# Expert weights turned once by DMA transposes from SBUF, instead of in both stages by TensorE

## What is computed

```python
x = x + 0.5 * _L0_ffn_ref(_layernorm(x), w_gate_up, w_proj)     # ternary FFN
x = x + _L0_attn_ref(_layernorm(x), w_qkv, w_out)               # 16 heads
x = x + 0.5 * _L0_ffn_ref(_layernorm(x), w_gate_up, w_proj)
x = x + 0.5 * _L1_ffn_ref(_layernorm(x), gate_w, gate_b, W1, W2, W3, Ws1, Ws2, Ws3)
x = x + _L1_attn_ref(_layernorm(x), W_Q, W_K, W_V)              # retention
x = x + 0.5 * _L1_ffn_ref(_layernorm(x), gate_w, gate_b, W1, W2, W3, Ws1, Ws2, Ws3)
```

```python
h = silu(einsum('td,eid->tei', xt, W1)) * einsum('td,eid->tei', xt, W3)   # 8 experts, 128 wide
y = einsum('tei,edi,te->td', h, W2, dw)                                   # dw: two experts per token
z = silu(xt @ Ws1.T) * (xt @ Ws3.T) @ Ws2.T                               # a ninth, shared
return y + z
```

## Time and profile before

| what | us |
|---|---|
| median of three runs (lowest, highest) | 1695.41 (1694.16, 1696.23) |
| the profiled execution's own time | 1694.91 |
| its span, first to last instruction | 1693.1 |
| TensorE busy | 1626.9, 96% of the span |
| VectorE, ScalarE, GpSimd busy | 1252.6, 1223.6, 1132.0 |
| first expert stage, from its first `up` | 1287.3 to 1443.1 |
| retention | 1443.1 to 1535.2 |
| second expert stage | 1535.8 to 1693.1 |

### The profile page before, as it was taken

One profiled execution on the slowest core, in us unless ns is written; L12 is line 12 of the kernel. 1 busy time (PEld: TensorE's weight loads), 2 busy tenths in 40 slices (PEclk: granted clock), 3 DMA queues, 4 the chain that ended last, 5 costly groups with the idle time before them and its releaser, 6 DMA issues.

```text
span 1693.1 us, 27014 instructions
## 1 busy us (share of the span) xinstructions
PE 1626.9 (96%) x9467; PEld 962.3 (57%) x9467; DVE 1252.6 (74%) x2407; ACT 1223.6 (72%) x1911; POOL 1132.0 (67%) x749
## 2 busy tenths in 40 slices
PE   4998999999999999999999999998999999999998
PEld 2565455555555555555555555554566566676665
DVE  7878777777777677777777777775796777977766
ACT  7867888988988988988888888885655443444432
POOL 1776888888888888888878878874664223663222
PEclk9999999999999999999999999999999999999999
DMA  9013778788779778788788788785001110000101
GB/s 296 1 51 63 139 129 154 128 143 171 126 146 168 125 150 160 129 152 162 125 152 153 125 143 149 131 139 111 1 1 60 55 53 1 1 2 29 29 10 51
DMA packets 580510, 174.07 MB, mean 103 GB/s; under 512 B 543244, under 2 KB 579351, under 8 KB 580247
## 3 DMA queue, kind: packets, MB, share of 16 engines
q1 hardware_dynamic: 580374, 172.33, 52.6%
HBM read 35.94 MB, written 2.10 MB: 22 GB/s over the span
## 4 chain that ended last, share of the span: by engine, by line
PE 78%; DVE 6%; ACT 2%; issue 1%; POOL 1%; SPq 0%; DMA 0%; DVEq 0%; ACTq 0%; POOLq 0%
PE banks L1909 24%; PE banks L1910 24%; PE banks L1911 24%; PE banks L1984 1%; PE banks L1985 1%; DVE X L1750 1%; DVE mo_h L1737 1%; PE banks L2021 1%; DVE nmax L1563 1%; PE banks L2022 1%; PE banks L1919 1%; PE banks L2076 1%; DVE XN L1258 0%; PE banks L2238 0%; DVE x L1264 0%
## 5 line engine op out<-in xcount | busy, mean ns | idle before, releaser
L762 POOL TENSOR_TENSOR Pl<-Pm,Ph 128x1024 f16<-128x1024 f32 x256 | 546.7, 2136 | 46.8 <-ACT Ph L1026 45.8
L1016 ACT ACTIVATE Pm<-banks,nbias,s_scale 128x1024 f32<-128x1024 f32 x256 | 308.1, 1204 | 120.8 <-DVE nbias L1565 120.8
L1563 DVE TENSOR_REDUCE nmax<-banks 128x1 f32<-128x1024 f32 x256 | 312.6, 1221 | 96.8 <-PE banks L1911 95.7
L1026 ACT ACTIVATE Ph<-Pm 128x1024 f16<-128x1024 f32 x256 | 268.5, 1049 | 1.3
L741 POOL TENSOR_TENSOR rp_b<-rp_s,rope 128x512 f32<-128x512 f32 x128 | 163.0, 1273 | 135.6 <-ACT rp_s L993 135.4
L1602 DVE SCALAR_TENSOR_TENSOR X<-banks,rinv,X 128x256 f32<-128x256 f32 x256 | 112.7, 479 | 157.8 <-PE banks L1911 157.8
L818 POOL TENSOR_TENSOR mT_lo<-mo_h,mT_hi 128x512 f16<-128x512 f32 x72 | 83.8, 1164 | 205.8 <-ACT mT_hi L1129 205.5
L1909 PE MATMUL banks<-PT_hi,V_hi 128*128 128x512 f16 x512 | 195.1, 381 | 3.1 <-DMA PT_lo<-Pl 3.1
L1909 PE MATMUL banks<-QK_hi 128*128 128x512 f16 x512 | 195.3, 381 | 1.2 <-DVE QK_lo L1650 1.2
L1910 PE MATMUL banks<-PT_lo,V_hi 128*128 128x512 f16 x512 | 195.1, 381 | 0.0
L1911 PE MATMUL banks<-PT_hi,V_lo 128*128 128x512 f16 x512 | 195.1, 381 | 0.0
(11 more groups left out here) (248 smaller groups left out, 4129.9 us busy)
## 6 DMA issues: line engine op xcount, KB each, us to landing
moe_raw<-in_L_ffn_W SPq DMA_DIRECT2D x72, 128.0 KB, 2.3
w_all<-in_L_attn_w_qkv SPq DMA_DIRECT2D x3, 2048.0 KB, 15.8
a_raw<-in_L_attn_w_qkv SPq DMA_DIRECT2D x24, 256.0 KB, 3.1
PT_hi<-Ph SPq DMA_TRANSPOSE x256, 3.4
PT_lo<-Pl SPq DMA_TRANSPOSE x256, 3.3
raw_gu<-in_L_ffn_w_gate_up SPq DMA_DIRECT2D x2, 1024.0 KB, 7.2
X<-in_L_attn_x SPq DMA_DIRECT2D x2, 1024.0 KB, 12.9
o_raw<-in_L_attn_w_out SPq DMA_DIRECT2D x8, 256.0 KB, 3.4
```

Of the source, the lines that this page charges most:

```text
L762: nc.gpsimd.tensor_tensor(Pl[:, z % 4, :], Pm[:, k, :], Ph[:, z % 4, :], ALU.subtract).then_inc(pl_done.sem, 1)
L1016: nc.scalar.activation(Pm[:, k, :], two_banks[z % 2][:], ACT.Exp, bias=nbias[:, z:z + 1], scale=s_scale[:], accum_out=rsum[:, z:z + 1]).th ...
L1026: nc.scalar.activation(Ph[:, z % 4, :], Pm[:, (base * SLOTS + z) % 3, :], copy).then_inc(ph_done.sem, 1)
L1563: nc.vector.tensor_reduce(nmax[:, z:z + 1], two_banks[z % 2][:], AX, ALU.max, negate=True).then_inc(max_done.sem, 1)
```

## The change

Weights are turned once, in the first expert stage, and kept for the second. ScalarE and VectorE split the raw rows in SBUF into `m16` (high and low part, one buffer); Sync then issues two DMA transposes of 128 x 768 fp16, one for each part, into `w16`, which holds all nine experts. TensorE's `expert_weights` and all waits that belonged to it are gone. The split of weight `q` waits for the transposes of `q - 1`, because `m16` is single. Work for weight 0 moves into the last phase of the FFN, and the later weights move to other steps. In the second expert stage no weight is loaded, split or turned. `r_raw`, `xpos`, `decay` and `at_hi` change their addresses in SBUF; the last two mixes of the retention return to banks 6 and 7.

```diff
-    w13_hi, w13_lo, w2_hi, w2_lo = [], [], [], []
...
+    w16 = sb("w16", [P, NX, 2, 3, D], fp16)
...
+    m16 = sb("m16", [P, 2, 3, D], fp16)
...
-        WEIGHTS_AFTER = {0: 2, 7: 3, 13: 4, 15: 5, 17: 6, 20: 7, 24: 8}
+        WEIGHTS_AFTER = {0: 2, 4: 3, 7: 4, 9: 5, 13: 6, 16: 7, 18: 8}
...
-        MIX_BANK = [(4, 5, 6, 7, 4, 5, 6, 7), (4, 5, 6, 7, 4, 5, 2, 3)]
+        MIX_BANK = (4, 5, 6, 7, 4, 5, 6, 7)
...
# Sync
                 if q >= 2:
-                    sp.wait_ge(mo_wT.sem, 2 * (q - 1))
+                    sp.wait_ge(mo_wlo.sem, 2 * (q - 1))
...
-            load_expert(2)
-            load_expert(3)
+            def turn_expert(e):
+                sp.wait_ge(mo_wlo.sem, 2 * (e + 1))
+                for part in range(2):
+                    sp.dma_start_transpose(out=w16[:, e, part].rearrange("p a (c i) -> p (a c) i", c=DC),
+                                           in_=m16[:, part].rearrange("p a d -> p (a d)")).then_inc(mo_wT_in.sem, 16)
+            for e in range(2):
+                turn_expert(e)
+                load_expert(e + 2)
 
             sp.wait_ge(x_added.sem, x_added.before(0, 3))
             for m, w in enumerate((W_Q, W_K, W_V)):
                 sp.dma_start(r_raw[:, m], w.rearrange("(c p) o -> p c o", p=P)).then_inc(ret_in.sem, 16)
-            for q in range(4, 2 * NX):
+            for q in range(4, NX):
+                turn_expert(q - 2)
                 load_expert(q)
...
+            for e in (NX - 2, NX - 1):
+                turn_expert(e)
# ScalarE
+                    if f and (phase, ht) == (3, 5):
+                        expert_weights_hi(0)
...
-                act.wait_ge(mo_wT.sem, 2 * q + 1)
-                nc.scalar.activation(w13_hi[q % LAG][:].rearrange("p a c i -> p (a c i)"), bank[6], copy,
-                                     scale=l_inv[:, 0:1]).then_inc(mo_whi.sem, 1)
...
+                act.wait_ge(moe_in[k % 2].sem, 48 * (k // 2 + 1))
+                if q:
+                    act.wait_ge(mo_wT_in.sem, 32 * q)
+                nc.scalar.activation(m16[:, 0, 0:2, :], moe_raw[:, k % 2, 0:2, :], copy, scale=l_inv[:, 0:1]).then_inc(mo_whi.sem, 1)
+                nc.scalar.activation(m16[:, 0, 2, :], moe_raw[:, k % 2, 2, :], copy, scale=l_inv[:, 1:2]).then_inc(mo_whi.sem, 1)
...
-                    if i in WEIGHTS_AFTER:
-                        expert_weights_hi(q0 + WEIGHTS_AFTER[i])
+                    if m == 0 and i in WEIGHTS_AFTER:
+                        expert_weights_hi(WEIGHTS_AFTER[i])
...
# VectorE: expert_weights_lo takes moe_raw and m16 in the same way
+                        if f and ht == 6:
+                            expert_weights_lo(0)
...
                 else:
-                    expert_weights_lo(0)
+                    expert_weights_lo(1)
...
-                    if f and j == 1:
-                        expert_weights_lo(1)
...
# TensorE: expert_weights and its calls are removed
-                    if c == 0:
-                        pe.wait_ge(mo_wlo.sem, 2 * (q + 1))
+                    if m == 0 and c == 0:
+                        pe.wait_ge(mo_wT_in.sem, 32 * (e + 1))
...
-                    elif t == TPH + 2 and b < B - 1:
+                    elif t == TPH + 2:
                         x_ready(of_x, l_next, 1)
```

More of the change, by code:

```diff
@@ L216, in build_program, with w13, w2 @@
     place["at"] = top_ffn
-    w13_hi, w13_lo, w2_hi, w2_lo = [], [], [], []
[L218 to L222, removed]
+    w16 = sb("w16", [P, NX, 2, 3, D], fp16)
+    xpos = sb("xpos", [P, 4, S], f32)
+    decay = sb("decay", [P, S], f32)
+    r_hi = sb("r_hi", [P, 3, DC, D], fp16)
+    r_lo = sb("r_lo", [P, 3, DC, D], fp16)
+    m16 = sb("m16", [P, 2, 3, D], fp16)
     top_moe = place["at"]
+    def w13(e, part):
+        return w16[:, e, part, 0:2, :].rearrange("p a (c i) -> p a c i", c=DC)
+    def w2(e, part):
+        return w16[:, e, part, 2, :]
     place["at"] = phase0
@@ L231, in build_program @@
     rv_hi = sb("rv_hi", [P, TT, D], f32r)
+    rv_lo_at = place["at"]
     rv_lo = sb("rv_lo", [P, TT, D], f32r)
[L233 to L240, removed]
     at_hi = sb("at_hi", [P, TT, HALF], f32r)
     top_ret = place["at"]
+    assert top_ret <= top_ffn
+    place["at"] = rv_lo_at
+    r_raw = sb("r_raw", [P, 3, DC, D], f32)
+    assert low_moe <= rv_lo_at and place["at"] <= top_ffn
     place["at"] = wffn_at
@@ L1399, in expert_weights_lo @@
             def expert_weights_lo(q):
+                k = N_NORM_LOADS + q
                 dve.wait_ge(mo_whi.sem, 2 * q + 1)
-                nc.vector.scalar_tensor_tensor(w13_lo[q % LAG][:].rearrange("p a c i -> p (a c i)"), bank[6], l_inv[:, 0:1],
-                                               w13_hi[q % LAG][:].rearrange("p a c i -> p (a c i)"), ALU.mult,
+                nc.vector.scalar_tensor_tensor(m16[:, 1, 0:2, :], moe_raw[:, k % 2, 0:2, :], l_inv[:, 0:1], m16[:, 0, 0:2, :], ALU.mult,
                                                ALU.subtract).then_inc(mo_wlo.sem, 1)
                 dve.wait_ge(mo_whi.sem, 2 * q + 2)
-                nc.vector.scalar_tensor_tensor(w2_lo[q % LAG][:], bank[7][:, 0:D], l_inv[:, 1:2], w2_hi[q % LAG][:],
+                nc.vector.scalar_tensor_tensor(m16[:, 1, 2, :], moe_raw[:, k % 2, 2, :], l_inv[:, 1:2], m16[:, 0, 2, :],
                                                ALU.mult, ALU.subtract).then_inc(mo_wlo.sem, 1)
@@ L1783, in experts @@
                         ln_lo(0, l + 1, 0)
-                    if i in WEIGHTS_AFTER:
-                        expert_weights_lo(q0 + WEIGHTS_AFTER[i])
+                    if m == 0 and i in WEIGHTS_AFTER:
+                        expert_weights_lo(WEIGHTS_AFTER[i])
                     if m == 0 and i in (14, 19, 22):
@@ L1890, in retention @@
                     add(t)
-                    if t >= TPH + 2 and b == B - 1:
-                        expert_weights_lo(NX + t - TPH - 2)
             ffn(0, 0)
@@ L2068, in ffn @@
                     down(len(PHASES) - 1, j)
-                    if f and j == 1:
-                        expert_weights(1)
             def weights(m, to):
@@ L2228, in attention @@
                 attention_pair("tail", NP)
[L2230 to L2237, removed]
-                        last = nc.tensor.transpose(bank[6][:, (a * DC + c) * EI:(a * DC + c + 1) * EI],
-                                                   moe_raw[:, k % 2, a, c * P:(c + 1) * P], ident[:])
-                last.then_inc(mo_wT.sem, 1)
-                for c in range(DC):
-                    last = nc.tensor.transpose(bank[7][:, c * P:(c + 1) * P], moe_raw[:, k % 2, 2, c * EI:(c + 1) * EI], ident[:])
-                last.then_inc(mo_wT.sem, 1)
             def experts(m, l):
@@ L2258, in up @@
                         for k in range(DC):
-                            last = split3(bank[2 * (i % 2) + a], w13_hi[q % LAG][:, a, k, :], w13_lo[q % LAG][:, a, k, :],
+                            last = split3(bank[2 * (i % 2) + a], w13(e, 0)[:, a, k, :], w13(e, 1)[:, a, k, :],
                                           x16[:, b, k, half, 0, :], x16[:, b, k, half, 1, :], k == 0, k == DC - 1)
@@ L2395, in mix @@
                         pe.wait_ge(r_atlo.sem, r_atlo.at(b, nh * TPH + mt + 1))
-                        last = split3(bank[MIX_BANK[b][t]][:, 0:D], at_hi[:, mt, q], at_lo[:, mt, q], rv_hi[:, mt, :], rv_lo[:, mt, :],
+                        last = split3(bank[MIX_BANK[t]][:, 0:D], at_hi[:, mt, q], at_lo[:, mt, q], rv_hi[:, mt, :], rv_lo[:, mt, :],
                                       mt == 0, mt == t)
@@ L2424, in retention @@
                     mix(t)
-                    if t >= TPH + 2 and b == B - 1:
-                        if t == TPH + 2:
-                            x_ready(of_x, l_next, 1)
-                        expert_weights(NX + t - TPH - 2)
             ffn(0, 0)
```

30 lines of the change are left out of this document (6 added, 24 removed).

## The result

The kernel after takes 1685.88 us in the median (1683.54 to 1686.27), where the kernel before took 1695.57 us (1694.16 to 1696.23) beside it: 0.9945 of the time, 95% interval 0.9930 to 0.9959. The prediction was 1685.1 us. The profiled execution took 1685.84 us with a span of 1684.0 us (before 1694.91 and 1693.1).

What follows compares the result with a forecast made beforehand. The prediction took TensorE, busy 96% of the span, as the bound. Its terms, -11.7 + 0.2 + 1.2 = -10.3 us, took the median from 1695.41 to 1685.1 us, range 1683.7 to 1687.0 (chance 0.60).

Steps and rivals of the forecast that it cites:

- The gain: On TensorE, both expert stages and retention: removing 18 turnings (108 transposes) saves 11.7 us with a stall-free replacement.
- The turning's length: Two DMA transposes take 4.7 us from VectorE's low part to last landing; bounds 3.5 and 7.8 us.
- rival B: Late turnings at up to 7.8 us a pair stall `up(1)` and later weights, 4 us in total, 1689; chance 0.17.
- the slack at `up(1)` and `up(4)`: First expert stage: weight 1 is turned 3.8 us before `up(1)`, weight 2 1.0 us before `up(4)`.
- the wait at step 9: First stage: ScalarE's split of weight 5 waits for weight 4, split at step 7: about 6 us against 4.7.
- C: Turning waits make it slower: whole gain gone near 10.3 us a pair; about 1725 us at 15.7; chance 0.05.
- The page's rule: Skill page: use TensorE where PSUM will do; by DMA 1309 ns a block, 15.7 us a turning; given little weight.
- Weight 3 at step 4: First stage: its moved low part delays product(5) and the additions the second `down` awaits; TensorE loses 1.2 us once.
- The router's chain: Step 2 of both stages: `up(5)` waits for VectorE, so part of step 0's gain is lost, 0.2 us in all.
- The step that failed: End of the FFN: weight 0's splits fit idle time on ScalarE and VectorE (1.31 us before the last product); cost nothing.
- The addresses: Changed SBUF addresses of buffers were taken to cost nothing.
- The sum: Whole kernel: -11.7 + 0.2 + 1.2 = -10.3 us, giving a median of 1685.1 us.

Runs made afterwards that it cites:

- w3_later: The kernel after with weight 3's split back behind step 7 of the first expert stage and the later splits moved along; 1684.00 us, 0.9939 of before.
- w0_earlier: The kernel after with VectorE's low part of weight 0 one FFN step earlier (ht 5 in place of 6); 1683.21 us, 0.9940 of before.
- turning_plus_one: The kernel after with one more DMA transpose issued and waited for ahead of each turning; 1687.90 us, 0.9966 of before.
- turning_plus_two: The kernel after with two more DMA transposes, each waited for, ahead of each turning; 1701.12 us, 1.0039 of before.

## Why the prediction was right

**The gain.** 18 turnings at 11.7 us, counted from start to start: shown. (Thirteen turnings, not fourteen, took 0.65 or 0.66 us, and TensorE's waits sum to 10.7 us in the trace, where it has some 12; neither changes the forecast.) The kernel without the other losses gives back 11.65 us. By the durations, 29.5 us, the forecast would have been far off.

**The turning's length.** 4.7 us taken, 4.3 us measured for weight 0, and up to 5.4 us in another kernel. No matmul waited for `w16`, so rival B did not happen. That the slack at `up(1)` and `up(4)` and the wait at step 9 are the places where it decides is shown by the longer turnings. The price of being late was too low in rivals B and C, since the clock adds to a wait.

**The page's rule.** Six blocks landed in 2.8 us in one DMA. The page "VectorE: DVE Perf Modes" of the Trainium skill, in "The three transpose paths", has 1309 ns for one block; twelve of them would make 15.7 us for a turning, an estimate from that page. The trace disagrees for a tile of many blocks, and it decides.

**Weight 3 at step 4.** +1.2 us forecast, at the second `down`, once, and in the first stage alone. Measured +1.07 us, there and nowhere else; `w3_later` takes it back. Right in place, cause and size.

**The router's chain.** +0.2 us forecast, nothing measured: with weight 3 back in its place the first stage gains all of its 4.60 us, and the second gains 4.63. The wait at `up(5)` is 1.50 us against 1.44.

**The step that failed.** "ScalarE's split falls in an idle stretch ... VectorE's ... fits the 1.31 us ... Cost: nothing", and with it "the nine splits themselves have the same durations from SBUF as from PSUM". It cost 0.94 us (0.74 by the second execution of the kernel after). The prediction had itself named low parts "much over 0.75 us beside GpSimd's work" as a sign of being wrong, and that came true: the median of the nine was 0.96 us. A low part from PSUM reads one operand from SBUF, one from `moe_raw` reads two. The pair of rows that shows it is weight 3's low part before, 0.75 us at 1317.98, and weight 4's after, each begun 0.74 us into the same GpSimd instruction. GpSimd in before, then VectorE and GpSimd in after:

```profile
1317.25 1.16 POOL L818 TENSOR_TENSOR mT_lo<-mo_h,mT_hi 128x512 f16<-128x512 f32 x1 [2.26 <-ACT mT_hi L1129]
```

```profile
1317.48 0.97 DVE L1415 SCALAR_TENSOR_TENSOR m<-moe_raw,l_inv,m 128x512 f16<-128x512 f32 x1
...
1316.74 1.16 POOL L832 TENSOR_TENSOR mT_lo<-mo_h,mT_hi 128x512 f16<-128x512 f32 x1 [2.27 <-ACT mT_hi L1145]
```

It ends 0.55 us after GpSimd's does (1317.90 and 1318.45), and so do three more of the nine (0.96 to 0.97 us each). The one of 1.75 us at the end of the FFN does the same: GpSimd ends at 1273.90, VectorE at 1274.45. The four that meet no GpSimd instruction took 0.73 to 0.75 us. At 0.73 us weight 0's would have let the product start at about 1273.8, by an estimate ahead of the 1274.1 that TensorE allows (its place in before, 2.80 us behind the `XN` transposes). The earlier trace rows had 0.74 us from SBUF, but at a time when GpSimd was not inside an instruction. The page "SBUF — State Buffer" of the Trainium skill, in "Who interferes with whom", says that a VectorE instruction with two inputs in SBUF contends with a GpSimd instruction that reads SBUF, that the ports which the two share are an exclusive lock, and that issue order decides who blocks. This trace agrees, with 0.54 to 0.55 us left after GpSimd's end all five times.

**The addresses.** Costed at nothing, they cost about 0.7 us in the retention, and the clock some 0.6 us more in the executions that had the half-clock stretch.

**The sum.** -11.7 + 1.07 + 0.94 + 0.7 = -9.0 us without the half-clock stretch, where the prediction had -10.3. The stages of the kernel after, with 0.6 us put back for that stretch, give -8.9; the medians -9.7 in one series and -8.9 in the other. The forecast of 1685.1 against 1685.88 is thus nearer than its terms deserve: the two missing terms, 0.94 and 0.7 us, are offset in part by the router's 0.2 us and weight 3's 0.1 us that were not lost, and in the profiled execution by 0.8 us in the work ahead, which is luck.

## What to carry to other kernels

Count what an engine gains from removed matmuls from start to start, and check the forecast stage by stage: an expert stage repeats to 0.03 us where the whole time spreads by 3. When an operand of a VectorE instruction moves from PSUM to SBUF, look up what GpSimd is doing at that moment and add the rest of GpSimd's instruction to its time. A DMA transpose is free behind a step or two of other work and dear at the head of a stage, where its whole length shows, with slower matmuls after it.

## What the runs showed of the hardware

- A VectorE `SCALAR_TENSOR_TENSOR` of 128x512 with two inputs from SBUF, begun inside a GpSimd addition or subtraction of SBUF tiles, ended 0.54 to 0.55 us after it: 0.96 to 0.97 and 1.75 us in place of 0.74. In `w0_earlier` GpSimd's addition at 1267.16, begun second, took 1.72 us; the same one took 1.26 in the kernel after.
- The three waits of TensorE of 3.6 to 3.8 us were each followed by a window at a granted clock of 0.50 to 0.65, that is wholly or mostly at 1.2 GHz. This cost 1.7 us behind the one of 3.59 us. The waits of 1.86 and 1.34 us in `turning_plus_one` and that of 2.03 us in `turning_plus_two` were followed by none; that of 2.08 us at the end of the FFN there was followed by one of 0.65, that of 1.5 us in the retention by one in some executions only.
- The same 78 fp32r matmuls of 256 columns took 9.40 or 9.09 us (the last 0.03 us of the instruction ahead included) with `at_hi` next to `rv_lo` in SBUF or, exchanged with `xpos`, above `w16`. The cause is open.
- A DMA transpose of 128 x 768 fp16 landed in 2.8 us, against 3.4 us for 128 x 1024 in the attention; single ones took up to 4.5 us in other executions, the second one of the kernel after among them.
